# Normalised graph convolution in fp32: one loop of wide chunks in two whole slots, for a ring of five half pieces with a narrow first and last chunk

## What is computed

```python
def reference(x, adj, u):
    keep = (u >= 0.1).astype(x.dtype)
    x_drop = x * keep / (1.0 - 0.1)
    return layernorm(x + jnp.matmul(adj, x_drop), axis=-1)   # mean and variance over D, eps 1e-5
```

## Time and profile before

| | before |
|---|---|
| median of three runs | 641.97 us |
| the profiled execution | 641.88 us |
| its span | 640.1 us |
| TensorE busy | 502.8 us (79%) |
| queue of the loads, share of 16 DMA engines | 98.8% |
| mean moved | 429 GB/s |
| granted TensorE clock, mean | 0.92 |

### The profile page before, as it was taken

How to read it: one execution, slowest core, us unless ns; L and a number is a source line. 1 busy time by engine, 2 the same in 40 slices (tenths; PEclk the granted TensorE clock), 3 DMA queues, 4 the chain that set the end, 5 groups by cost and what they waited for, 6 DMA issues and landing times.

```text
span 640.1 us, 5097 instructions
## 1 busy us (share of the span) xinstructions
PE 502.8 (79%) x2312; PEld 179.7 (28%) x2312; DVE 53.7 (8%) x102; ACT 17.7 (3%) x41; POOL 1.6 (0%) x14
## 2 busy tenths in 40 slices
PE   0097969688799578879878689867869868689997
PEld 0062213232233222223222223222323223133344
DVE  1930001010010100101000010100101001010101
ACT  0001000000000000000000000000000000000000
POOL 1000000000000000000000000000000000000000
PEclk9997979988799978889979899978999969799999
DMA  9999999999999999999999999999999999999998
GB/s 393 459 394 455 431 420 454 405 446 439 422 421 436 435 451 422 438 408 444 459 418 434 442 412 455 420 434 446 426 418 426 446 451 422 438 405 438 425 425 364
DMA packets 7207, 274.84 MB, mean 429 GB/s; under 512 B 800, under 2 KB 928, under 8 KB 1312
## 3 DMA queue, kind: packets, MB, share of 16 engines
q1 hardware_dynamic: 7056, 272.63, 98.8%
q10 hardware_dynamic: 144, 2.10, 0.8%
HBM read 272.63 MB, written 2.10 MB: 429 GB/s over the span
## 4 chain that ended last, share of the span: by engine, by line
DMA 62%; PE 33%; DVE 3%; another core or an unknown queue 1%; issue 0%; ACT 0%; SPq 0%; DVEq 0%; ACTq 0%
DMA ring<-adj 56%; PE acc L202 33%; DMA ring<-adj_last 5%; DMA xdrop<-u 2%; DVE node_sum L317 1%; DVE xdrop L321 1%; DVE xdrop L329 1%; PE folded L210 0%; DVE x_sb L321 0%; PE lifted L237 0%; SPq L126 0%; ACT squares L303 0%; PE lifted L263 0%; ACT std L308 0%
## 5 line engine op out<-in xcount | busy, mean ns | idle before, releaser
L202 PE MATMUL acc<-ring,xdrop 128*64 128x512 f32 (+1 forms) x2176 | 485.6, 606 | 103.1 <-DMA ring<-adj 101.7
L202 PEld LDWEIGHTS acc<-ring,xdrop 128*64 128x64 f32 x2176 | 162.8, 146 | 413.0 <-issue 280.2
L344 DVE SCALAR_TENSOR_TENSOR y<-folded,x_sb 128x256 f32<-128x256 f32 (+1 forms) x16 | 6.7, 416 | 552.3 <-PE folded L210 552.3
L237 PE MATMUL lifted<-x_sb,lift 128*128 128x64 f32 x4 | 1.1, 428 | 30.6 <-DVE x_sb L321 30.6
L210 PEld LDWEIGHTS folded<-fold,sums_T 128*128 128x128 f32 x128 | 15.5, 191 | 12.6 <-issue 12.6
L284 ACT COPY sums_T<-acc 128x512 f32<-128x512 f32 x15 | 8.8, 585 | 335.0 <-PE acc L202 335.0
L210 PE MATMUL folded<-fold,sums_T 128*128 128x64 f32 x128 | 17.7, 281 | 0.0
L277 ACT ACTIVATE std<-square_sum,eps 128x4 f32<-128x4 f32 (+1 forms) x16 | 4.8, 297 | 225.2 <-DVE square_sum L351 225.2
L237 PEld LDWEIGHTS lifted<-x_sb,lift 128*128 128x128 f32 x4 | 0.9, 322 | 30.5 <-issue 30.5
L348 DVE TENSOR_TENSOR squares<-y 128x256 f32<-128x256 f32 (+1 forms) x16 | 6.7, 417 | 0.5
L355 DVE TENSOR_TENSOR x_sb<-y,rstd 128x256 f32 (+1 forms) x16 | 6.7, 416 | 0.6
(11 more groups left out here) (23 smaller groups left out, 5.5 us busy)
## 6 DMA issues: line engine op xcount, KB each, us to landing
ring<-adj SPq DMA_DIRECT2D x13, 4096.0 KB, 31.3
ring<-adj SPq DMA_DIRECT2D x2, 2048.0 KB, 28.7
xdrop<-u ACTq DMA_DIRECT2D x1, 2048.0 KB, 12.5
x_sb<-x SPq DMA_DIRECT2D x1, 2048.0 KB, 12.3
out<-x_sb SPq DMA_DIRECT2D x1, 1984.0 KB, 12.7
ring<-adj_last SPq DMA_DIRECT2D x1, 1920.0 KB, 29.5
ring<-adj_last SPq DMA_DIRECT2D x1, 1792.0 KB, 33.4
ring<-adj_last SPq DMA_DIRECT2D x1, 1536.0 KB, 30.6
```

Source lines behind the costliest of these rows:

```text
L202: last = nc.tensor.matmul(acc[i][D * h:D * h + D, 0:cols], xdrop[:, k, :], piece[:, b, :], start=(k < 2), stop=(k >= NB - 2))
L344: nc.vector.scalar_tensor_tensor(out=y[:, 0:nj, :], in0=folded[:, 0:nj, :], scalar=1.0 / KEEP, in1=x_sb[:, bass.ds(block0, nj), :], op0=AL ...
```

## The change

- The narrow chunks go (`NARROW` = 1). All 16 chunks are 512 columns wide and run in one loop of 16 rounds on TensorE.
- The ring goes. There are two slots, `pieces[0]` and `pieces[1]`, each for one whole 8 MB piece (32 blocks, 64 KB for each partition), one for the first and one for the second half of each chunk. A load is issued when the slot's piece has been used entirely (`piece_used`).
- Only the last chunk's two pieces come in parts: the first in 19 and 13 blocks, the second in 9, 7, 6, 4, 3, 2 and 1. The waits on the parts stand in the loop's body for all chunks; their semaphores are set so far ahead by GpSimd that they are open until the last chunk.
- There is one accumulator for three. TensorE waits for the copy of the last chunk's sums ahead of a chunk's first product. The first fold is of a zeroed `sums_T`.
- The fold of chunk c - 1 stands between chunk c's two pieces.
- The products begin after all four quarters of `xdrop` (before: quarter by quarter).
- `lifted` holds four blocks for two, so the end has four copies, four folds and four squares, the last multiply is 128 x 256, and the last store 128 KB.

```diff
-NARROW = 2
+NARROW = 1
-PARTS = (15, 14, 12, 9, 6, 5, 3)
+PARTS = ((19, 13), (9, 7, 6, 4, 3, 2, 1))
-        ring = sb("ring", [P, RING * HALF, COLS])
+        pieces = [sb(f"piece{s}", [P, PB, COLS]) for s in range(SLOTS)]
-        acc = [pb(f"acc{i}", [P, COLS]) for i in range(3)]
+        acc = pb("acc", [P, COLS])
@@ sync
+            def load(c, s):
+                sp.dma_start(pieces[s][:, :, :], adj[c * SLOTS + s, :, :, :]).then_inc(piece_in[s], 16)
+
+            for s in range(SLOTS):
+                load(0, s)
+            with sp.Fori(1, CHUNKS - 1) as c:
+                for s in range(SLOTS):
+                    sp.wait_ge(piece_used, c * SLOTS + (s + 1 - SLOTS))
+                    load(c, s)
+            for s in range(SLOTS):
+                sp.wait_ge(piece_used, FINAL * SLOTS + s + 1 - SLOTS)
+                for n, (k, size) in enumerate(parts[s]):
+                    arrived = part_in[s][n - 1] if n else piece_in[s]
+                    sp.dma_start(pieces[s][:, k:k + size, :], adj_last[s, :, k:k + size, :]).then_inc(arrived, 16)
@@ gpsimd
+            for n, arrived in enumerate(part_in[0] + part_in[1]):
+                nc.gpsimd.memset(late_free[:, n:n + 1], 0.0).then_inc(arrived, FINAL * 16)
+            nc.gpsimd.memset(sums_T[:, :], 0.0).then_inc(sums_copied, 1)
@@ tensor
+            def multiply(c, s):
+                for n, (k0, size) in enumerate(parts[s]):
+                    if n:
+                        pe.wait_ge(part_in[s][n - 1], c * 16 + 16)
+                    else:
+                        pe.wait_ge(piece_in[s], c * 16 + 16)
+                    for b in range(k0, k0 + size):
+                        k = s * PB + b
+                        h = k % 2
+                        last = nc.tensor.matmul(acc[D * h:D * h + D, :], xdrop[:, k, :], pieces[s][:, b, :],
+                                                start=(k < 2), stop=(k >= NB - 2))
+                last.then_inc(piece_used, 1)
...
+                pe.wait_ge(dropped, QUARTERS)
+                with pe.Fori(0, CHUNKS) as c:
+                    pe.wait_ge(sums_copied, c + 1)
+                    multiply(c, 0)
+                    for j in range(J):
+                        last = nc.tensor.matmul(folded[:, j, :], sums_T[:, j * P:j * P + P], fold[:, :],
+                                                start=True, stop=True)
+                    last.then_inc(folded_ready, 1)
+                    multiply(c, 1)
+                for j in range(LAST_J):
+                    pe.wait_ge(last_copied, j + 1)
+                    nc.tensor.matmul(lifted[:, j, 0:D], sums_T[:, j * P:j * P + P], fold[:, :],
+                                     start=False, stop=True).then_inc(last_folded, 1)
@@ scalar
+            with act.Fori(0, FINAL) as c:
+                act.wait_ge(piece_used, c * SLOTS + SLOTS)
+                act.wait_ge(folded_ready, c + 1)
+                nc.scalar.copy(sums_T[:, :], acc[:, :]).then_inc(sums_copied, 1)
                 spread(c)
+            act.wait_ge(piece_used, CHUNKS * SLOTS)
+            act.wait_ge(folded_ready, CHUNKS)
             for j in range(LAST_J):
+                nc.scalar.copy(sums_T[:, j * P:j * P + P], acc[:, j * P:j * P + P]).then_inc(last_copied, 1)
+
+            for j in range(LAST_J):
+                act.wait_ge(last_folded, j + 1)
                 nc.scalar.activation(squares[:, j, :], lifted[:, j, 0:D], ACT.Square,
                                      accum_out=square_sum[:, j:j + 1]).then_inc(last_var, 1)
```

More of the change, by code:

```diff
@@ L34 @@
 EPS = 1e-5
-PARTS = (15, 14, 12, 9, 6, 5, 3)
+PARTS = ((19, 13), (9, 7, 6, 4, 3, 2, 1))
+LATE = sum(len(sizes) - 1 for sizes in PARTS)
 def graph_layernorm(nc, x, adj, adj_last, u, out):
@@ L71, in graph_layernorm @@
         rstd = sb("rstd", [P, J])
-        acc = [pb(f"acc{i}", [P, COLS]) for i in range(3)]
+        acc = pb("acc", [P, COLS])
         folded = pb("folded", [P, J, D])
[L75 to L89, removed]
+        lifted = pb("lifted", [P, LAST_J, BANK])
+        parts = [[(sum(sizes[:n]), size) for n, size in enumerate(sizes)] for sizes in PARTS]
+        piece_in = [sem(f"piece_in{s}") for s in range(SLOTS)]
+        part_in = [[sem(f"part_in{s}_{n}") for n in range(1, len(parts[s]))] for s in range(SLOTS)]
         x_in = sem("x_in")
         u_in = sem("u_in")
-        half_used = sem("half_used")
-        last_done = sem("last_done")
+        piece_used = sem("piece_used")
         sums_copied = sem("sums_copied")
-        half_copied = sem("half_copied")
+        last_copied = sem("last_copied")
+        last_folded = sem("last_folded")
         folded_ready = sem("folded_ready")
@@ L196, in _ @@
         def _(pe):
[L197 to L231, removed]
@@ L234, in _ @@
[L234 to L260, removed]
@@ L269, in _ @@
+            program()
         @block.scalar
@@ L327, in _ @@
             dve.wait_ge(u_in, 16)
-            for q in range(HALVES):
+            for q in range(QUARTERS):
                 nc.vector.scalar_tensor_tensor(out=xdrop[:, quarter(q), :], in0=xdrop[:, quarter(q), :], scalar=P_DROP,
```

89 lines of the change are left out of this document (32 added, 57 removed).

## The result

The changed kernel takes 662.97 us (median of six runs, 660.5 to 669.77), the kernel before 641.83 in the same runs: a ratio of 1.034 (95% interval 1.029 to 1.038), 21 us slower. Forecast were 644.5, with a range of 643.2 to 647.1. Its profiled execution took 663.23 us, with a span of 661.4.

A forecast was written before the change was run, and what follows sets the result against it. The DMA load stream was taken to bound the kernel. Against the profiled 641.88 us, +1.7 at the end and +0.85 in the tail gave +2.55, with rounding 644.45, said as 644.5; range 643.2 to 647.1.

The forecast's parts named there:

- What bounds the kernel: Most of the span: the DMA stream sets the pace, queue at 98.8%; TensorE has 4 to 5 us slack per row.
- two slots for two and a half: Slot refills: 16.55 + 0.4 + 1.6 = 18.6 us, under 19.35, so refilled in time at no cost.
- The late-refill rival: Slot refills: a piece over 18.6 us leaves the DMA engines idle; 647 to 655 us, chance 0.08.
- The stream of loads: Loads: same bytes, fewer wrapped rows and split loads; last landing at 634.2 us, bounds 0 and -0.8.
- the end: Last two pieces: TensorE owes 42.4 us, the stream 39.2; products end at 637.5, 3.3 behind the last landing, +1.7 us.
- the tail: After the last products: two more folds and squares, a larger multiply and a larger last store, +0.85 us.
- The lower clock at the last whole piece: Last whole piece runs at the lower clock: +1.7, up to +2.6 us, 646.2 us; chance 0.25.
- One late DMA engine less: Early loads: fewer instruction fetches delay an engine, landings up to 1.1 us sooner; 643.4 us, chance 0.13.
- Refetch in each round: TensorE's loop: instructions fetched 16 times over, each delaying one engine by 1.1 us; +1.1, 645.6 us, chance 0.04.

The follow-up runs named there:

- the probes: Changed kernel with 5 and 3 added TensorE products per chunk, 1 or 2 of each moved ahead of the slot's release: 655.01 us (one), 675.97 us (two).
- the 5-and-3 run: Changed kernel with 5 added products ahead of each chunk and 3 behind each fold on TensorE: 653.7 us.
- the forecast's own case: Changed kernel with 5 and 3 added products in chunks 1 to 14 only, and one square root ahead of ScalarE's loop: 645.88 us.
- 24 blocks: Changed kernel with only 24 of each piece's 32 blocks multiplied, all loads kept: 641.06 us.
- the finer end: Changed kernel with half loads issued per used half slot, last chunk's first piece in 16, 8, 8 blocks, one square root ahead of ScalarE's loop: 644.73 us.

## Why the prediction was wrong

**What bounds the kernel**: right, and it is why the loss is so large. A stream at 98.8% has no place to catch up; each us that a refill is late stays.

**The step that failed is "two slots for two and a half"**, in its bound for the start of a transfer. I took 1.6 us, from issue to landing of the 64 KB store at the very end, and called it a bound from above. It is one for a small store on an idle queue only: at that point nothing else ran. In the changed kernel the refill issued at 169.83 began on its first DMA engine 0.95 us later, inside the bound, but on its last engines 3.6 us later, and it landed 2.2 us late. In the probes 4.4 us of lead were enough, and 3.65 weren't each time. The sum 16.55 + 0.4 + 1.6 = 18.6, "under 19.35", should have read 16.55 + 0.2 + 4.4 = 21.15 (a lead counts from the issue, so it holds the issue's own 0.4), which is over it by 1.8. Even a piece at the full clock, 13.95 + 0.2 + 4.4 = 18.55, has 0.8 us to spare and no more. So it takes both: a late start of the loads, and a late release. In the changed kernel the lower clock makes the release late: it takes 1.5 to 3 us in 24 of the 32 pieces. Without it the late start costs nothing (the 5-and-3 run); with a lead of 4.4 for 5.2 still nothing; with one more added product ahead of the release it costs 21 us more.

The row was there to warn me. In before the shortest time from issue to landing is 22.0, and I noted that before "was never near"; that was the reason to see that no row of before showed a short lead on a busy queue, and that the bound from above had to be open. The late-refill rival had the mechanism, its place, and a time of 647 to 655 at a chance of 0.08. Its point of decision, a piece over 18.6 us, was wrong even by its own terms: 18.6 is the sum with issue and start in it. With the 1.6 it is 19.35 - 0.4 - 1.6 = 17.35 us, a loss of 3.4 us in a piece and not 4.65, against 2.6 seen; with 4.4 it is under 15. The 662.97 measured lie outside this rival's time too.

**The stream of loads, the end and the tail** were right. In the forecast's own case the last landing of all is at 634.3 (634.2), TensorE ends 4.1 us behind it (3.3) and the tail is 2.9 (3.0). The difference at the end is a wait that I had costed at nothing: with one accumulator TensorE waits 0.76 us for ScalarE's copy at the last chunk. It is covered by idle time everywhere but there. In the changed kernel it is 2.12 us, since ScalarE loads its table first (the row at 625.79), and the run behind it takes 15.65 for 13.95, at a granted clock of 0.89.

The account of the changed kernel against the forecast's 637.5 for the end of the products, which came at 642.40 + 13.95 = 656.35: the last whole piece starts at 609.72 for 595.04, 14.7 us; the copy with its table load 2.1; the lower clock 1.7. The rest, 0.35, is rounding and the 0.2 us for a run, which the forecast counted once and not three times. The late refills are 14.7 of the 18.85.

**The other rivals.** The lower clock at the last whole piece didn't fall on that piece (13.95 at 609.72) but on the next one. One late DMA engine less: the instruction queue's packets did fall from seven to one, but the one that stayed was again in the first 60 us, and with it one late landing (51.69 to 72.32 with 24 blocks, 52.91 less 32.50 in the earlier trace rows). Refetch in each round: one packet in 16 rounds, so this is out as well. The Trainium skill's rule on taken branches ("Runtime: NRT & Kernel Launch", Instruction fetch mechanics) is for a target outside the current window of two pages, of 256 instructions each by the same section. A round of this loop has 274 products and weight loads by the page of the profile (4384 in 16 rounds), so it can lie within two pages, and the prediction was wrong to make this rival the forecast by that rule; this kernel doesn't test it.

**What stays open**: why a load begins so late on some engines, the last of them 2.6 us after the first though they are idle, and why its first packets take longer. Only the size was measured, for loads of 8 MB on SyncE's queue. Why the engines are further out of step in the changed kernel wasn't tested either. Whether fewer or smaller descriptors ahead would shorten it, or another queue, wasn't tried. The Trainium skill ("DMA: Bandwidth & Descriptors", Latency and other measured facts) gives 0.6 us to the first byte, and for HBM's latency 0.2 us on average and 2 us at high load. The first packet after the issue at 169.83 began 0.95 us behind it, of the order of the 0.6; 3.6 us to the last engine stand in no row of it.

## What to carry to other kernels

In a kernel bound by its loads, a slot must be refilled before the load ahead lands, by the time that a load needs to begin on all DMA engines and by how far these are out of step: here 4.4 us were enough with engines 1.2 us apart, 3.65 were not each time, and in the changed kernel even 4.6 lost 0.4. Take that time from a row at which the queue is full, and if there is none, leave the bound open. Count the lower clock into the time until the release, and let products begin on part of a slot: with each load split in two and the wait for the whole slot left as it was, that gave back 17 of the 21 us.

## What wasn't expected of the hardware

- A load of 8 MB needed about 4 us of lead, against 1.6 us for a whole small store on idle engines: its first packets began 0.95 to 3.6 us after the issue and took up to 3.5 us for 2.42.
- An added product of 128x512 cost 0.83 us (5 of them 4.46 and 3 of them 2.79 in the 5-and-3 run, so (4.46 - 2.79) / 2 each), but the kernel's own cost 0.43. The kernel's products go in turns to the upper and the lower 64 partitions of the accumulator; the added ones all go to the lower 64. The Trainium skill ("TensorEngine Tiling (Array Packing)", Key Properties) says that different tiles of the array can load weights and multiply in parallel; the two rows fit that, but no run here changed the halves alone.
- ScalarE's table load took 1.28 us, and a copy and a square root in turns in a loop reloaded a table ahead of each in every round. In before, which had used both ahead of its loop, and with one square root ahead of the loop in the finer end, there are no loads in the loop. The page of before, then of the finer end:

```profile
L290 ACT ACT_TABLE_LOAD x1 | 1.3, 1283 | 49.4 <-PE acc L202 49.4
L277 ACT ACT_TABLE_LOAD x1 | 1.3, 1283 | 0.0
```

```profile
L212 ACT ACT_TABLE_LOAD x1 | 1.3, 1283 | 1.2 <-PEq L300 1.2
```
